# Retention layer on one core: scores as four 32-row tiles from unstacked operands, six abs buffers, two of four step pairs added by accumulating DMAs

## The reference, cut to what matters

```python
q = (xf @ Wq.T); k = (xf @ Wk.T * SCALING); vr = (xf @ Wv.T)      # 8 heads of 32 channels
qr = theta_shift(q, sin_q, cos_q)
kr = theta_shift(k, sin_k, cos_k)
qk = jnp.einsum('bhqd,bhkd->bhqk', qr, kr) * mask[None]           # 1024 x 1024 for each head
den = jnp.clip(jnp.abs(qk).sum(-1, keepdims=True), 1.0, 50000.0)
out = jnp.einsum('bhqk,bhkd->bhqd', qk / den, vr)
```

## Time and profile before

| what | value |
|---|---|
| median of 3 runs | 2471.46 us (2471.05 to 2474.01) |
| the profiled execution | 2479.87 us, its span 2478.1 us |
| mean granted TensorE clock | 0.993 |
| stage of the retention layer | the first 1020 us, 32 phases |

### The profile page before, as it was taken

How to read it: one execution, slowest core, us unless ns; L and a number is a source line. 1 busy time by engine, 2 the same in 40 slices (tenths; PEclk the granted TensorE clock), 3 DMA queues, 4 the chain that set the end, 5 groups by cost and what they waited for, 6 DMA issues and landing times.

```text
span 2478.1 us, 36390 instructions
## 1 busy us (share of the span) xinstructions
PE 2437.3 (98%) x13326; PEld 1688.8 (68%) x13326; DVE 1855.7 (75%) x2772; ACT 1464.8 (59%) x2063; POOL 999.8 (40%) x695
## 2 busy tenths in 40 slices
PE   8999999999999999999999999999999999999999
PEld 4444444444444444699899878888888888888887
DVE  5888888888888888777777667777666667767775
ACT  3676767676767676666666455555555555555554
POOL 3787777777777777314332301111111100111110
PEclk9999999999999999999999989999999999999999
DMA  7222323232323233244454340000000000000000
GB/s 250 51 78 68 86 69 86 69 86 69 86 69 85 69 86 87 73 66 91 75 93 82 52 111 26 26 26 26 26 26 26 26 26 26 17 17 19 26 26 17
DMA packets 117058, 149.91 MB, mean 60 GB/s; under 512 B 32769, under 2 KB 74121, under 8 KB 116625
## 3 DMA queue, kind: packets, MB, share of 16 engines
q1 hardware_dynamic: 116352, 146.87, 23.5%
q10 hardware_dynamic: 528, 0.72, 0.1%
HBM read 71.93 MB, written 25.26 MB: 39 GB/s over the span
## 4 chain that ended last, share of the span: by engine, by line
PE 89%; DVE 6%; issue 2%; ACT 1%; DMA 1%; POOL 0%; SPq 0%; DVEq 0%; POOLq 0%
PE scores L445 10%; PE scores L1766 9%; PE scores L1768 9%; PE scores L1767 9%; PE pairC L458 8%; PE pairC L475 6%; PE pairD L379 3%; DVE l_prod L586 3%; PE pairC L1766 2%; PE pairC L1767 2%; PE pairC L1768 2%; PE pairD L1766 2%; PE pairD L1768 2%; PE pairD L1767 2%; PE pairD L388 2%
## 5 line engine op out<-in xcount | busy, mean ns | idle before, releaser
L586 DVE TENSOR_TENSOR l_prod<-scores,l_window 128x1024 f32<-128x1024 f32 x512 | 613.6, 1217 | 142.2 <-PE scores L445 134.3
L799 ACT ACTIVATE l_absp<-l_prod 128x1024 f32<-128x1024 f32 x512 | 540.2, 1056 | 293.4 <-DVE l_prod L586 283.6
L445 PE MATMUL scores<-l_qst,l_kst 96*128 96x512 f32 x1024 | 380.9, 462 | 14.0 <-DVE l_prod L586 10.9
L1925 ACT ACTIVATE e_r<-scores,e_bn,e_rs 128x512 f32<-128x512 f32 x256 | 197.9, 779 | 276.7 <-PE scores L1768 276.6
L2156 POOL TENSOR_TENSOR e_xnorm<-e_res,e_scale 128x1024 f32<-128x1024 f32 x16 | 38.5, 2404 | 775.9 <-DMA e_res<-t2T_scratch 775.9
L445 PEld LDWEIGHTS scores<-l_qst,l_kst 96*128 96x128 f32 x1024 | 164.9, 190 | 272.9 <-DVE l_prod L586 132.1
L915 POOL TENSOR_TENSOR l_absp<-l_absp,l_absp 128x1024 f32<-128x1024 f32 x126 | 297.8, 2384 | 14.3 <-ACT l_absp L799 14.0
L2032 DVE CAST e_h1hi<-e_r 128x512 fp32r<-128x512 f32 x256 | 144.0, 563 | 208.2 <-ACT e_r L1925 207.9
L1935 ACT ACTIVATE e_r<-scores,e_bn,e_rs 128x512 f32<-128x512 f32 x250 | 195.1, 781 | 138.8 <-PE scores L1768 137.3
L458 PE MATMUL pairC<-l_prod,l_v 128*32 128x512 f32 x2048 | 268.1, 595 | 0.5 <-ACT l_tA L803 0.5
L2059 DVE TENSOR_TENSOR e_r<-e_r,e_wbc 128x512 f32<-128x512 f32 x250 | 170.9, 690 | 86.2 <-ACT e_r L1935 85.9
(11 more groups left out here) (249 smaller groups left out, 4982.8 us busy)
## 6 DMA issues: line engine op xcount, KB each, us to landing
l_kst<-l_hi SPq DMA_DIRECT2D x248, 64.0 KB, 2.0
l_qst<-l_hi SPq DMA_DIRECT2D x248, 64.0 KB, 2.0
l_xo<-in_x SPq DMA_DIRECT2D x32, 256.0 KB, 3.0
x_scratch<-l_xo SPq DMA_DIRECT2D x32, 256.0 KB, 2.4
l_xa<-x_scratch SPq DMA_DIRECT2D x8, 1024.0 KB, 8.2
l_xr<-x_scratch SPq DMA_DIRECT2D x8, 1024.0 KB, 5.5
t2T_scratch<-l_xt SPq DMA_DIRECT2D x8, 1024.0 KB, 14.9
e_scale<-rows_scratch SPq DMA_DIRECT2D x16, 512.0 KB, 4.1
```

Of the source, the lines that this page charges most:

```text
L445: mm = nc.tensor.matmul(sc[j][:, s, :], kst[g][0:96, h, 128 * kt:128 * kt + 128], qst[c][0:96, h, :], start=True, stop=True)
L586: nc.vector.tensor_tensor(prod[2 * (S % 2) + j][:], sc[j][:], win[:, 4 * g + 2 * j:4 * g + 2 * j + 2, w0:w0 + QC], ALU.mult).then_inc(prod ...
L799: nc.scalar.activation(absp[S % ABS][j][:], prod[2 * (S % 2) + j][:], ACT.Abs).then_inc(abs_ready, 1)
L1925: nc.scalar.activation(r1[:, m, :], p1[m], ACT.Relu, bias=bn_[0][1][:, m, n:n + 1], scale=rs[0][:, m, n:n + 1]).then_inc(r1_ready, 1)
```

## The change

Scores: `kst`, `qst`, `hi` and `lo` go, and so do all stacking DMAs and their semaphores. ACT and POOL write the high and low parts straight into `khi`, `klo`, `qhi` and `qlo`, in which head h lies on partitions 32h to 32h + 31. `scores(S)` now has no j: it issues 12 matmuls of 32 rows, for each of the three products one for each head, each head in its own row tile of the array and its own PSUM bank. It runs once in an iteration, before both halves of the side task, and waits for both products of the step before. DVE does both products of a step one after the other, and what stood between them comes behind them. The ring of abs tiles has six slots. POOL issues two accumulating DMAs in a phase that add the abs tiles (1 MB each) of the pairs at kt 0 and kt 4; `sums` then runs four times. `clip_den` keeps the scaled denominators in PSUM, clips from there, and PE waits for the clipped ones (`den_ready`).

```diff
-    ABS = 4
-
-    def pairs(P):
+    ABS = 6
+
+    def by_dma(P):
+        return (0, 4) if P < PHASES - 1 else (0,)
+
+    def by_pool(P):
         return (2, 6) if P < PHASES - 1 else (2,)
...
-            return {2: (0,), 3: (1,), 5: (2, 3), 6: (4,), 7: (5,), 9: (6, 7)}
+            return {5: (0, 1), 6: (2, 3), 8: (4, 5), 9: (6, 7)}
...
-        def scores(S, j):
+        def scores(S):
...
             if S > 0:
-                pe.wait_ge(prod_ready, 2 * S + j - 1)
-            for s in range(2):
-                h = 2 * j + s
-                mm = nc.tensor.matmul(sc[j][:, s, :], kst[g][0:96, h, 128 * kt:128 * kt + 128], qst[c][0:96, h, :],
-                                      start=True, stop=True)
+                pe.wait_ge(prod_ready, 2 * S)
+            for n, (k, q) in enumerate(((khi, qhi), (klo, qhi), (khi, qlo))):
+                for h in range(4):
+                    rows = slice(32 * h, 32 * h + 32)
+                    mm = nc.tensor.matmul(sc[h // 2][:, h % 2, :], k[g][rows, 128 * kt:128 * kt + 128], q[c][rows, :],
+                                          start=(n == 0), stop=(n == 2))
             mm.then_inc(scores_ready, 1)
...
-                if S + 1 < KT * PHASES:
-                    scores(S + 1, part)
+                if S + 1 < KT * PHASES and part == 0:
+                    scores(S + 1)
...
-            dve.wait_ge(scores_ready, 2 * S + j + 1)
+            dve.wait_ge(scores_ready, S + 1)
...
             products(S, 0)
+            products(S, 1)
...
-            nc.vector.tensor_tensor(dent[:], nT_A[:, :, 0], scales[:, 0, P % 4, :], ALU.mult).then_inc(den_scaled, 1)
+            nc.vector.tensor_tensor(nT_A[:, :, 0], nT_A[:, :, 0], scales[:, 0, P % 4, :], ALU.mult).then_inc(den_scaled, 1)
             dve.wait_ge(den_scaled, P + 1)
-            nc.vector.tensor_scalar(dent[:], dent[:], 1.0, 50000.0, ALU.max, ALU.min).then_inc(den_ready, 1)
+            nc.vector.tensor_scalar(dent[:], nT_A[:, :, 0], 1.0, 50000.0, ALU.max, ALU.min).then_inc(den_ready, 1)
...
+        def dma_pair(S):
+
+            pool.wait_ge(abs_ready, 2 * (S + 1) + 2)
+            pool.dma_start(absw[(S + 1) % ABS][:].rearrange("p j s q -> p (j s q)"),
+                           absw[S % ABS][:].rearrange("p j s q -> p (j s q)"), accum_op=ALU.add).then_inc(dma_added[S % KT], 16)
```

More of the change, by code:

```diff
@@ L211, in layer0 @@
     pair_added = sem("pair_added")
+    dma_added = {kt: sem(f"dma_added{kt}") for kt in by_dma(0)}
     a_ready, b_ready = sems("a_ready b_ready")
@@ L230, in layer0, with prepared @@
     NMADE = 3
[L232 to L250, removed]
+    def prepared(n):
+        if n % 2 == 0:
+            c = (n // 2 + 1) % 2
+            return qhi[c][:], qlo[c][:]
+        P = n // 2
+        g, part = (P // 2 + 1) % 2, slice(QC * (P % 2), QC * (P % 2) + QC)
+        return khi[g][:, part], klo[g][:, part]
     r.xo_out, r.prod_ready, r.n_taken, r.d_taken, r.den_done = xo_out, prod_ready, n_taken, d_taken, den_done
-    r.den_scaled, r.o_added, r.centred, r.idn = den_scaled, o_added, centred, idn
+    r.den_ready, r.o_added, r.centred, r.idn = den_ready, o_added, centred, idn
     r.PHASES, r.STEPS, r.UNITS, r.OUTS = PHASES, KT * PHASES, len(units), len(o_order)
@@ L269, in sync @@
             sp.dma_start(dst, src).then_inc(consts, 16)
[L271 to L281, removed]
-        sp.wait_ge(first_hi, K0 + 1)
-        first_stack(sp, K0, (0, 2), range(4))
-        sp.wait_ge(first_hi, Q0 + 1)
-        first_stack(sp, Q0, (1,), range(1, 4))
-        sp.wait_ge(first_lo, Q0 + 1)
-        first_stack(sp, Q0, (2,), range(2, 4))
-        sp.wait_ge(first_hi, K1 + 1)
-        first_stack(sp, K1, (0, 2), range(4))
-        sp.wait_ge(first_lo, K1 + 1)
-        first_stack(sp, K1, (1,), range(4))
+        sp.wait_ge(first_hi, K0 + 1)
         sp.dma_start(win[:, H // 2:H], window[:, H // 2:H]).then_inc(window_in, 16)
@@ L362, in a_free @@
             else:
[L363 removed]
+                pe.wait_ge(den_ready, before[1] + 1)
         def b_free(task):
@@ L498, in tensor @@
         busy(6)
-        scores(0, 0)
-        scores(0, 1)
+        scores(0)
         pe.wait_ge(consts, 16 * NCONST)
@@ L777, in take, with high @@
             nc.scalar.activation(t1[:], pA[:], ACT.Copy, scale=scale).then_inc(t1_ready, 1)
-        def high(n, stacks, count):
-            if stacks is not None:
-                act.wait_ge(stacks, count)
+        def high(n):
             act.wait_ge(sum_ready, n + 1)
-            nc.scalar.activation(hi[:], t1[:], ACT.Copy).then_inc(hi_ready, 1)
+            nc.scalar.activation(prepared(n)[0], t1[:], ACT.Copy).then_inc(hi_ready, 1)
         def v_take(a, g, half):
@@ L794, in absolute @@
             if before >= 0:
-                if before in pair_steps:
+                if before in dma_steps:
+                    act.wait_ge(dma_added[before % KT], 16 * (before // KT + 1))
+                elif before in pair_steps:
                     act.wait_ge(pair_added, 2 * pair_of[before] + j + 1)
@@ L945, in gpsimd @@
         for P in range(PHASES):
-            if P > 0 and 6 in pairs(P - 1):
-                add_pair(KT * (P - 1) + 6, 0)
-                add_pair(KT * (P - 1) + 6, 1)
+            if P > 0:
+                pair(P - 1, 6)
+            pair(P, 0)
             if has_q(P):
@@ L957, in gpsimd @@
                 rotated(prep_k(P))
+            pair(P, 4)
             if P > 0:
```

89 lines of the change are left out of this document (43 added, 46 removed).

## The result

The changed kernel takes 2486.06 us (median of 5 runs, 2482.92 to 2487.61), the old one 2473.02 on the same chip (5 runs, 2471.05 to 2474.01): ratio 1.0047, 95% interval 1.0034 to 1.0059. It is 13 us slower. The forecast was 2479 in a range of 2455 to 2570, slower.

The account below looks back on a forecast made before the run. PE bounds the old kernel; after the change each iteration lasts the longer of PE's need and the 3.46 us PE-DVE turn. +15 over 30 phases and -8 at the start, on 2471.5, give 2479 us, range 2455 to 2570.

Parts of the forecast that it names:

- Turn: PE-DVE handover per iteration: scores wait for both products, then products for all scores; 3.46 us, DVE idle 1.10 of it.
- Scores by row tiles: A step's twelve matmuls run as three side-by-side rounds of 0.215 us, 0.88 us with the entry from another tile shape.
- The switch to full tiles: From row-tile scores to a side task in full tiles on PE: costs 0.23 us, bounds 0 and twice that.
- rival under 0.09: Row-to-full-tile switch nearly free: kt 0, 4 and 6 shorter by 0.2 each, -20 us, 2459, faster; chance 0.22.
- The phase: One retention phase takes 31.5 to 31.6 us instead of 31.06: +0.5, over 30 phases +15 us.
- the group statistics: Second phase of an image, kt 7: four small DVE operations feed a matmul of the next iteration, +0.95 us, an estimate.
- iteration 5 of the third kind: kt 5 in an image's third phase: a second output projection makes it PE's, 4.45 us, +1.0.
- the turn in place of 3.82 in the fourth kind: kt 4 in an image's fourth phase has no projection: -0.25 us.
- The first phase: Waits for stacks and `raw` and the slow clock behind them all go: -8 us, bounds -2 and -10.
- the first scores' wait: Start of the kernel: the first scores' wait of 2.01 us for the stacks goes, 2.0 of the 8 us gained.
- The clip: DVE clip at kt 3 takes 0.17 us from PSUM, just covered; at 1.85 it would cost 1.7 a phase, +50 us.
- ACT, POOL, DMA: ACT covered at some 22 us a phase, POOL reaches 27; DMA issues 1 to 1.5 us, landing 8 to 11, hidden.

Follow-up runs that it names:

- run 1: The changed kernel without its two accumulating DMAs, all six sums of denominators per phase standing again: 2484.9 us.
- run 3: The changed kernel with the sum over steps 2 and 3 moved from iteration 6 to iteration 7: 2460.7 us.
- run 7: The changed kernel with each score-times-window product over 512 of its 1024 columns from step 4 on: 2411.6 us.
- run 5: The old kernel with only the change's clip, scaled denominators kept in PSUM and clipped from there: 2472.4 us.
- run 8: The old kernel with each score-times-window product over 512 of its 1024 columns from step 4 on: 2453.7 us.
- run 2: The changed kernel with the denominators' scale and clip written to SBUF as in the old one: 2526.7 us.
- run 6: The changed kernel with a ring of four abs tiles in place of six: 2582.9 us.
- run 9: The old kernel with the accumulating DMAs, a ring of six abs tiles and the window cut to two heads: 2461.5 us.
- run 11: The old kernel with accumulating DMAs, ring of six, window cut to two heads and PSUM clip, at kt 3 moved between the two products: 2441.8 us.

## Why the prediction came out as it did

**Direction and mechanism: right.** PE's gain of two sums goes into waits for DVE. Turn 3.44 (forecast 3.46), DVE idle of 0.96 and about 1 us, PE's waits for products 83.6 us, no wait for the DMA: as forecast. Of the waits before scores 30 stand in iteration 3 (31.8 us), 29 in iteration 0 (25.6) and 24 in 5 and 6 (21.5), that is mainly behind the iterations 2, 7 and 5 that the prediction gives to the turn. Runs 1, 3 and 7 show the mechanism by intervention, not only by trace.

**Scores by row tiles: right.** Chain 0.91 (forecast 0.88), rounds 0.23 behind the first (0.215). The Trainium skill, "TensorE: Matmul & The Clock Gate", Part 3, gives 3.07 times for four row tiles; here it is more by an estimate, 4 x 0.215 / 0.23 = 3.7 times, if a matmul alone takes the 0.215 of the prediction; no run times one alone.

**The switch to full tiles: a little too dear.** The projection behind row tiles has 1.91 in the chain, 2 x 0.86 in the earlier trace rows: 0.19; transposes 0.59 against 0.44: 0.15. Forecast 0.23, rival under 0.09. The rival's price is excluded by these rows. That a change of tiling mode drains TensorE (the Trainium skill, "TensorEngine Tiling (Array Packing)", Key Properties) agrees with the 0.15 to 0.19.

**The phase: +0.5 forecast, +0.17 measured; this is the term that was mis-sized.** By kind I had 31.1, 31.75, 32.65 and 30.55 (30.8 with each kind's extra); measured are 30.87, 31.01, 32.63 and 30.40. The second kind was to be 0.68 longer than the first (+0.95 for the group statistics against +0.27) and is 0.14 longer: PE waits for `gvar` (L617) 0.3 each time. Where the rest went was not followed. The first and fourth kinds are 0.20 and 0.15 under the forecast, about what the cheaper switch gives in three projections and a few transposes (an estimate). Two slips of the sum nearly cancel: with the switch, iteration 5 of the third kind is 4.68 and not 4.45, and the turn in place of 3.82 in the fourth kind is -0.36 and not -0.25. So 24 middle phases cost 4 us, not 12.

**The first phase: -8 forecast; the step was wrong.** It took the stall of one profiled execution, at its full length and with the slow clock behind it, for the kernel's. In the profiled pair the first `weighted` starts at 34.93 instead of 36.24 and the first four phases take 126.24 us against 126.50, so 1.6 of the 8 us were gained there. Against run 5's execution of nearly the old kernel (first `weighted` at 37.64, four phases 119.92) the same stretch loses 3.6 us. The first phase alone takes 33.95 us in the profiled execution of the old kernel, 28.76 in run 5's and 29.18 in run 8's, and 31.04 in the changed kernel. Run 8's execution has the stall too (its products are halved from step 4 on):

```profile
56.55 0.73 PE L445 MATMUL scores<-l_qst,l_kst 96*128 96x512 f32 x2 [1.85 <-DVE l_prod L587]
```

So the wait is the old kernel's, but 1.00, 1.85 or 3.69 us long, and the clock fell behind the longest alone. Nor is the 2.0 us of the first scores' wait shown as a gain: the first `weighted` starts at 36.24 to 37.97 in four executions with the old start, and at 33.94 to 37.12 in seven with the new one.

The profiled execution is also why the profiles differ by 4.2 us and the medians by 13: the old kernel's profiled execution lay 7 us above its median. I corrected for that (8.4 us, from the three runs then known) and then counted the same stall once more as a gain of the change.

The start isn't smooth after either. Its row in the changed kernel's timeline:

```profile
31.02 0.51 PE L418 MATMUL scores<-l_qhi,l_khi 32*128 32x512 f32 x4 [2.63 <-DVE l_prod L560]
```

PE stands 2.63 us for the first products, with no half of a step in hand. In three stretches of this kernel PE is busy throughout, and the clock is partly at its lower level (1.2 GHz against 2.4), so that its mean is well under 1:

```profile
32.00:37.00 5.00, 5.00 (x20) 1.44 (x24) 3.10 (x4) 2.60 (x3) 0.11 (x1) 0.66 0.55 206
107.00:112.00 5.00, 5.00 (x24) 1.29 (x16) 3.35 (x8) 2.97 (x5) 4.39 (x2) 0.66 0.48 188
985.00:989.00 4.00, 4.00 (x11) 3.19 (x12) 2.50 (x4) 2.11 (x2) 0.14 (x1) 0.58 0.00 2
```

The old kernel has 0.68 in the first, so that one is not the change's; it has 1.00 in the second and the third. The third lies in the 31st phase. The phases 29 to 31 take 94.00 us against 90.89 in run 5's execution; in run 1's, where the clock stays up, the 31st takes 30.96 instead of 32.37, so the fall stands for about 1.4 of these 3.1 us.

So the forecast was +15 - 8 = +7. Against run 5's execution the changed kernel loses 3.6 us up to the end of the fourth phase, 3.3 in the 24 middle phases and 3.1 in the three after them, and is 1.5 us shorter behind those: together 8.5, the difference of the two executions (2482.3 and 2473.8). The medians of the two kernels are 13.7 apart (2486.1 and 2472.4), because the changed kernel's execution lay 2.0 under its median and run 5's 3.2 over. That 2479 stands as near to 2486 as it does is luck: too much in the middle and too little at both ends nearly cancel.

**The clip: right**, 0.17 and covered; the price at 1.85 was put at 50 us and is 41 (run 2). "At 1.85 it would cost" was true only of the changed kernel (run 5).

**ACT, POOL, DMA: right with six tiles.** Landing 7.1 us (estimate 8 to 11), issue 0.90 (1 to 1.5). What I didn't see is how near the ring is to being the bound: two tiles fewer cost 97 us (run 6). It is the row tiles that make room for them, by freeing the stacks.

**What stays open.** Why the clock falls at 985 to 989 us in the changed kernel, and why behind some waits and not behind others like them: in run 9's two undisturbed phases PE waits as long (0.66 and 1.02) as in the four with a fall. No run has the scores in row tiles and in halves, or the old scores joined, so what joining the halves costs is read from the waits and from runs 7 and 8, not from an edit of that alone. What holds run 11's phase 0.6 us above what the sums alone would give was not followed. The start of the old kernel is known from few executions.

## What to carry to other kernels

- Before an operation is taken off the engine that is busy all the time, ask in which iterations that engine stands above the next bound. Two sums fewer, with iterations of 2.54 us left under a turn of 3.44, gave nothing; a sum moved out of an iteration of 4.68 us into one of 2.54 gave 25 us.
- Splitting a step's scores in halves was the buffer between PE and DVE. A change that joins the halves makes the latencies, 1.1 us here, and DVE's 2.36 of work part of each iteration.
- The length of a wait seen in one execution is no property of the kernel (3.69, 1.85 and 1.00 us here): look at a second execution, and don't take it off the median and off the profile both.

## What the runs showed of the hardware

- A DMA that adds 1 MB from SBUF to SBUF lands in 7.1 us and takes POOL 0.90 us to issue; plain 1 MB DMAs of the earlier trace rows take 5.5 and 14.9.
- A 16-column clip on DVE takes 0.175 us from PSUM while POOL works, and 2.05 (run 2) or 1.85 from SBUF, where it ends 0.03 to 0.04 us after POOL's pair sum; from SBUF with POOL idle it takes 0.17. That agrees with the Trainium skill, "SBUF — State Buffer", practical consequences, on the port that DVE and GpSimd share.
- Four loads of 32 rows take 0.19 us together, as long as one load of 96 rows.
- Two equal phases with and without a fall of the granted clock (0.57 over 227 to 231 us) differ by 1.4 us (run 9).
